# Transformer block on one core: one first-FFN stage moved ahead of the first gates, and the later stage order shifted

## What is computed

```
x = x + attention(layernorm(x))            # 32 heads of 16, causal
x = x + ffn(layernorm(x))                  # "f1": dequantised weights, 1792 wide
x = x + topk_mlp(layernorm(x))             # 1376 wide, see below
x = x + ffn(layernorm(x))                  # "f2": the same weights as f1
ffn(y)      = (silu(y @ gate) * (y @ up)) @ down
topk_mlp(y) : s = silu(y @ w_gate.T); in each row the 688 elements of s that are smallest in |s| are set to 0;
              result = (s * (y @ w_up.T)) @ w_down.T
```

## Time and profile before

| | |
|---|---|
| median of 3 runs | 2002.21 us (2000.06 to 2006.18) |
| span of the profiled execution | 2000.6 us |
| TensorE busy | 1867.0 us, 93% of the span |
| VectorE busy | 1487.5 us, 74% |
| ScalarE busy | 1038.1 us, 52% |
| GpSimd busy | 635.2 us, 32% |
| mean granted clock of TensorE | 0.983 |

### The profile page before, as it was taken

How to read it: one execution, slowest core, us unless ns; L and a number is a source line. 1 busy time by engine, 2 the same in 40 slices (tenths; PEclk the granted TensorE clock), 3 DMA queues, 4 the chain that set the end, 5 groups by cost and what they waited for, 6 DMA issues and landing times. The chain is left out here.

```text
span 2000.6 us, 40100 instructions
## 1 busy us (share of the span) xinstructions
PE 1867.0 (93%) x15312; PEld 1158.9 (58%) x15312; DVE 1487.5 (74%) x2424; ACT 1038.1 (52%) x1973; POOL 635.2 (32%) x812
## 2 busy tenths in 40 slices
PE   7998888998889789999999999999999999999989
PEld 3443333333334467775775766766676776757756
DVE  6567787888863215987888889888898898978931
ACT  4334777777773114644645636535635635546411
POOL 4685756576752111121112112121131121211221
PEclk9998999999999889999999999999999999999999
DMA  7875455455534403004030040132211121041000
GB/s 245 238 200 146 131 131 153 111 152 158 147 110 149 151 1 114 1 29 142 1 114 25 33 135 1 58 118 74 84 52 58 38 87 58 1 141 40 12 11 12
DMA packets 127215, 183.19 MB, mean 92 GB/s; under 512 B 46480, under 2 KB 83344, under 8 KB 127072
## 3 DMA queue, kind: packets, MB, share of 16 engines
q1 hardware_dynamic: 121072, 165.22, 27.0%
q0 software_dynamic: 4272, 12.91, 1.9%
q10 hardware_dynamic: 1728, 3.15, 0.4%
HBM read 147.39 MB, written 33.62 MB: 90 GB/s over the span
## 5 line engine op out<-in xcount | busy, mean ns | idle before, releaser
L1411 POOL TENSOR_TENSOR lohi<-h,lohi 128x256 f16<-128x256 f32 x224 | 173.7, 776 | 873.8 <-ACT lohi L1563 873.6
L1552 ACT ACTIVATE kept<-ax,T 128x1376 f16<-128x1376 f32 x248 | 357.0, 1439 | 122.5 <-DVE T L1626 116.6
L1620 DVE TENSOR_SCALAR_CACHE_REDUCE junk<-ax,T 128x1376 f16<-128x1376 f32 x248 | 406.4, 1639 | 2.7
L1067 ACT ACTIVATE pr<-s 128x512 f32<-128x512 f32 (+2 forms) x640 | 320.2, 553 | 94.7 <-PE s L956 73.9
L649 DVE TENSOR_REDUCE mx<-s 128x2 f32<-128x1024 f32 (+2 forms) x300 | 320.0, 1113 | 62.2 <-PE s L628 33.3
L1449 PE MATMUL ga<-xT_f,w_gate 128*128 128x256 f16 x2688 | 332.8, 274 | 7.5 <-DVE h L1677 4.6
L1459 PE MATMUL acc<-w_down,lohi 128*128 128x512 f16 x1344 | 326.4, 379 | 9.1 <-POOL lohi L1411 9.0
L1449 PE MATMUL ub<-xT_f,w_up 128*128 128x256 f16 x2688 | 332.2, 274 | 0.0
L1449 PEld LDWEIGHTS ga<-xT_f,w_gate 128*128 128x128 f16 x2688 | 262.9, 98 | 80.0 <-DVE h L1677 7.2
L1449 PEld LDWEIGHTS ub<-xT_f,w_up 128*128 128x128 f16 x2688 | 263.8, 98 | 31.9
L1677 DVE SCALAR_TENSOR_TENSOR h<-ub,g 128x256 f32<-128x256 f32 x224 | 94.1, 420 | 165.6 <-ACT g L1558 164.6
(11 more groups left out here) (177 smaller groups left out, 2668.0 us busy)
## 6 DMA issues: line engine op xcount, KB each, us to landing
ring<-wgu_scr SPq DMA_DIRECT2D x64, 688.0 KB, 5.3
ring<-wd_scr SPq DMA_DIRECT2D x24, 768.0 KB, 4.7
wgu_scr<-tk_h POOLq DMA_DIRECT2D x32, 172.0 KB, 2.8
q_scr<-qk_h SPq DMA_DIRECT2D x16, 256.0 KB, 2.6
k_scr<-qk_h SPq DMA_DIRECT2D x16, 256.0 KB, 4.4
v_scr<-v_f SPq DMA_DIRECT2D x16, 256.0 KB, 5.4
Q<-q_scr SPq DMA_DIRECT2D x64, 64.0 KB, 2.0
K<-k_scr SPq DMA_DIRECT2D x64, 64.0 KB, 2.0
```

The source lines that it names most:

```text
L1067: nc.scalar.activation(pr[:, g % NPR, NP * t + p0:NP * t + p1, 0:w], scores, ACT.Exp, scale=SCALE).then_inc(e2_ok, 1)
L1411: nc.gpsimd.tensor_tensor(hT[j % 2][:, 1, :], h[j % 2][:, :], hT[j % 2][:, 0, :], ALU.subtract).then_inc(hl_ok, 1)
L1552: nc.scalar.activation(kept[0][:, :], ax[k % 2][:, 1, :], ACT.Sign, scale=-1.0, bias=TF[:, 1:2], accum_out=cnt[:, 1:2]).then_inc(c1_ok, 1)
L1620: nc.vector.tensor_scalar(junk[:, :], ax[k % 2][:, 0, :], TF[:, 0:1], -float(KZERO), ALU.is_lt, ALU.add, accum_out=cnt[:, 0:1]).then_inc(c ...
```

## The change

```diff
-FFN_ALONE = (3, 6)
+FFN_ALONE = (2, 4, 6)
 
 
 def mlp_order(NC):
 
-    ffns = [("f1", 1), ("f1", 2)]
+    ffns = [("f1", 2)]
     for k in range(NC - 3):
         ffns += [("f1", k + 3), ("f2", k)]
     ffns += [("f2", NC - 3), ("f2", NC - 2)]
-    order = [("f1", 0), ("gates", 0)]
+    order = [("f1", 0), ("f1", 1), ("gates", 0)]
     for k in range(NC):
         first, second = ffns[0], ffns[1] if k not in FFN_ALONE else None
```

## The result

The changed kernel takes 2016.36 us (median of 5 runs, 2014.05 to 2019.03) against 2000.74 us of the kernel before in the same session: a ratio of 1.0076, with a 95% interval of 1.0056 to 1.0096. It is slower by 0.8%, and the forecast was 2016 with a range of 2007 to 2028. The profiled execution has a span of 2014.6 us, 14.0 above that of before.

A forecast was written before the change was run, and what follows sets the result against it. The prediction took PE to bound the kernel, with DVE close behind. Its terms, -9.1 + 16.4 + 3.7 + 3 = +14 us, on the 2000.6 us span gave 2014.6; 1.6 more for the median made 2016 us, range 2007 to 2028.

The forecast's parts named there:

- Part 1: Behind f1 0: the exposed norm goes, as f1 1 follows and hosts are found for the norms; minus 9.1 us.
- Part 2: Behind down 0 and down 1: two new exposed norms come, 8.2 us each; plus 16.4 us.
- Part 3: In the downs: four follow gates instead of three, and these are dearer; plus 3.7 us, between 1 and 6.
- Part 4: In the FFNs: the search has less PE cover, so DVE products come late; plus 3 us, between -4.6 and +10.
- Nothing for the queues: In SP's and POOL's queues: chunk stores and the loads behind them stay hidden, no added time.
- DVE as the bound: Rival: DVE bounds the single-FFN periods, adding 15 to 20 us to Part 4; 2024 to 2036 us, chance 0.14.
- Not slower: Rival: each new exposed norm costs under 6 us and DVE is nowhere late; 2002 us, chance 0.06.
- Small cost: Rival: exposed norms at 7 us each, or DVE late no more than now; 2004 to 2008 us, chance 0.08.

The follow-up runs named there:

- e6: The changed kernel with matmuls whose result nobody reads put into its three exposed norms: 2007.49 us, ratio 1.0021.
- e5: The changed kernel with each search bit counting over 344 of the 1376 columns: 1994.84 us, ratio 0.9954.
- e10: The changed kernel with the one-element subtraction L1642 taking its second operand as a per-partition scalar, not a second tensor: 2015.2 us, ratio 1.0064.
- e4: The kernel before with each search bit counting over 344 of the 1376 columns: 1982.13 us, ratio 0.9877.
- e11: The kernel before with unread matmuls in both exposed norms and at the MLP phase's start, and no search item in a down's first two slots: 1990.33 us.
- e2: The changed kernel with f2 0 and f1 4 exchanged, leaving one new exposed norm: 2015.09 us, ratio 1.0058.
- e1: The kernel before with only f1 1 moved ahead of gates 0: 2025.3 us, ratio 1.009.
- e3: The changed kernel with f2 0 and f1 4 exchanged and gates 3 ahead of f2 1, no new exposed norm: 2005.05 us, ratio 1.0005.

## Why the prediction was right, point by point

**Part 1 (-9.1).** From the start of f1 0 to down 0 the phase takes 236.8 us before and 282.4 after, with one FFN more: 55.7, the length of a second FFN in a pair (108.8 less 53.1), less the 0.9 of the transposes that left gates 1. That leaves -9.2. The hosted norms cost nothing that shows.

**Part 2 (+16.4).** From the end of the last product to the third group: 993.78 - 982.07 = 11.7 and 1171.38 - 1158.96 = 12.4, less 2.6 and 0.8 each: 8.3 and 9.0, so 17.3. The waits of 3.95 us are those of down 7 to the hundredth, and both paid the clock, as e6 shows from the other side. The second is dearer because the clock had fallen ahead of its transposes (1.97 us in place of 1.11). The rule of the Trainium skill, TensorE: Matmul & The Clock Gate, "What's actually happening", left open that they might not pay it; in this profile both did.

**Part 3 (+3.7).** The downs without the FFN products come to +3.4, but by other amounts. (Twelve of 18 matmuls in 4.24 us would be 2.8 us, not the 2.7 of the prediction; by the distances of their starts they take 2.6, which is used here. This changes the sum by 0.1.) Down 1 was mis-sized most: 26.4 less 2.6 = 23.8 up to its end, where I had 21.0. It begins with a wait of 2.66 us for POOL's low parts of f1 4, and PE falls to the half clock behind it. With shorter bits this wait is gone (e5); without the held subtraction it is longer, 3.44 us (e10). So it comes from how the bits stand at the end of f1 4, and not from the 2.61 us wait near its begin:

```profile
1137.34 2.64 PE L1459 MATMUL acc<-w_down,lohi 128*128 128x512 f16 x6 [2.66 <-POOL lohi L1411]
1141.29 0.87 PE L1488 MATMUL d_tr<-ident,pp 128*128 128x128 f32 x3 [1.31 <-DVE lohi L1692]
1141.96 3.27 PE L1501 MATMUL acc<-ring,lohi 128*128 128x512 f16 x9
```

The four downs behind gates made this good: all four kept the full clock and took 21.8 where I had 22.5. That is luck: in the versions of this study with the full search and items in a down's first slots 13 of 34 such downs had the half clock, with the same two waits, and took up to 22.9 where the others took 21.8. About 1 us each comes with the execution. The larger miss is one of cause: e4 and e11 show that what I took for a property of the order (nothing between the first turned tile and its product) is 1.8 us of search bits out of 2.5.

**Part 4 (+3).** FFN stages beyond their plain length (53.1 us, and 52.2 for f1 4 after the change, which has no norm to host): before 0.9 + 2.3 + 1.2 + 2.3 (f2 0, f2 1, f1 6, f1 7) = 6.6; after 4.5 + 2.6 + 2.6 (f1 4, f2 2, f1 7) = 9.7, so +3.1. The wait itself grew from 4.6 to 6.4 us, where I had 7.5; the slow groups behind the 2.61 us wait made up the difference. f1 4 was first, then f2 2 and f1 7 alike, as said. That f1 3 and f2 1 cost next to nothing is right too. One reading under this part was wrong: the six waits of the earlier trace rows do not lie in the four stages with the most finishing items. f2 0 and f1 6 carry 18 of them and have 0.48 us each; f2 1 and f1 7 carry five and have 1.8 each; f2 6 carries 18 and has none. What counts is which items stand just ahead of a product, as e4 and f1 4 show, and not their number.

Sum: -9.2 + 17.3 + 3.4 + 3.1 = 14.6, against 14.8 in the profiles. The chain of waits was foreseen; that the total came out to within 1 us of the forecast of 14 is closer than the method allows, because dear and cheap places (the second exposure and down 1, against the four downs behind gates) cancelled.

**Nothing for the queues** held for this change. e2 shows how near it was: with one FFN exchanged, the same queue cost 9 us.

**The rivals.** *DVE as the bound* falls: it wanted 15 to 20 us more in part 4, which came out at +3.1, and with bits half as long the change still costs 8.4 us (e5 against e4). It would be right for the order of e1, where DVE's lateness costs 31.4 us. *Not slower* falls with two exposures at 8.3 and 9.0, where it wanted under 6. *Small cost* would have needed one of these bounds as well.

## What to carry to other kernels

In a software pipeline written out by hand, count at each border whether the next stage reads what this one just produced: each such place costs the whole latency of its chain and the half-clock stretch behind it (8 to 9 us here). Taking one away helps only if nothing else waits in its place (e2: 8.3 us gained at one stage, 9 lost at another). Cover for a serial side job is a budget, and one taken from a single period costs far more than the same amount spread. Before a wait is put down to the order of the stages, look at what stands ahead of the wanted operation in the other engines' queues; here moving the planner's items out of two slots of each down brought 5 us, and the reordering brought none in any of its forms (at best e3: 2.4 us by the profile, nothing by the medians).

## What the runs showed of the hardware

A DVE operation with two tensors from SBUF was held for as long as POOL's masking ran: one element per row took 2.71 us beside a masking of 2.78, 0.15 with POOL idle, and 0.21 beside a masking with its second operand as a per-partition scalar (e10). The reverse is seen too: POOL's low part, 0.67 us in most of its runs, took up to 2.87 beside DVE's scan L1665. The Trainium skill, SBUF — State Buffer, "Reading the diagram", says that the two engines share a port pair under an exclusive lock, and that on DVE's side operations with two SBUF inputs are among those that take it, against a GpSimd operation that reads SBUF; the masking and the low part both read SBUF, and these numbers agree. The bit's small operation L1624 has only one tensor as input, yet it takes 0.72 us in place of 0.23 when POOL's low part runs beside it. Whether it takes the pair in another way no run here shows; this stays open.

Eight transposes between two waits did not keep the clock up. Behind down 0 they still ran at the full clock (1.11 us), and then the granted clock is 0.50 from 988 to 994 us; behind down 1 it had fallen ahead of them (1.97 us) and is 0.50 from 1162 to 1171 us. With nineteen plain matmuls in the same two waits (e6) it is 1.00 throughout. A single wait of about 2.7 us can go either way: the clock fell behind the 2.66 us in down 1 of the changed kernel, and not behind the 2.73 us at the same place in e6.
